# Adding a layer's bias to its nodes by accumulating DMAs of POOL in place of VectorE's additions

## What is computed

```
layer 0:  out = (d * (adj + I) * d) @ x @ W0^T + b0
layer 1:  att[i, j] = softmax_j( p . relu(q[j] + k[i]) + mask(adj) );  out = att @ x      (no bias)
layer 2:  out = (d * (adj + I) * d) @ (x @ W2) + b2
layer 3:  out = (d * adj * d) @ x @ W3 + b3
```

## Time and profile before

| | |
|---|---|
| Median of 3 runs | 14031.23 us (14029.29 to 14034.36) |
| Profiled execution | 14031.93 us, of which the span of the instructions is 14030.1 us |
| TensorE clock granted, mean | 0.982 of full speed |
| DMA | 935.48 MB, all issued by SP; the hardware queue q1 takes 20.9% of the 16 DMA engines |
| HBM | 65 GB/s over the span |

### The profile page before, as it was taken

One profiled execution on the slowest core, in us unless ns is written; L12 is line 12 of the kernel. 1 busy time (PEld: TensorE's weight loads), 2 busy tenths in 40 slices (PEclk: granted clock), 3 DMA queues, 4 the chain that ended last, 5 costly groups with the idle time before them and its releaser, 6 DMA issues. The chain is left out here.

```text
span 14030.1 us, 318060 instructions
## 1 busy us (share of the span) xinstructions
PE 13002.6 (93%) x143877; PEld 5489.3 (39%) x143877; DVE 13269.3 (95%) x13964; ACT 13100.1 (93%) x8612; POOL 1060.3 (8%) x699
## 2 busy tenths in 40 slices
PE   7889989999899998999989999999989999899988
PEld 3333434444344433444334443344433444333333
DVE  6999999999999999999999999999999999999995
ACT  5999999999999999999999999999999999999994
POOL 0000000010000100001000100001000010000000
PEclk8999999999999999999999999999999999999999
DMA  5111112221122111221122211222112221011103
GB/s 187 46 51 47 49 53 83 86 66 51 55 85 90 61 43 62 88 88 58 39 72 86 86 58 40 72 83 87 58 36 75 90 80 58 30 50 52 43 12 109
DMA packets 714332, 935.48 MB, mean 67 GB/s; under 512 B 61712, under 2 KB 455952, under 8 KB 693520
## 3 DMA queue, kind: packets, MB, share of 16 engines
q1 hardware_dynamic: 712976, 915.13, 20.9%
HBM read 722.01 MB, written 184.55 MB: 65 GB/s over the span
## 5 line engine op out<-in xcount | busy, mean ns | idle before, releaser
L1055 DVE TENSOR_SCALAR big<-q_pair,k_pair_cols 128x2048 f32<-128x2048 f32 x10036 | 12122.4, 1283 | 426.5 <-PE score L1203 409.1
L815 ACT ACTIVATE big<-q_f,k_cols 128x2048 f32<-128x2048 f32 x6144 | 11792.8, 1998 | 320.5 <-PE score L1203 275.3
L1203 PE MATMUL score<-big,unit_window 128*32 128x512 f16 x81920 | 5181.7, 396 | 708.5 <-DVE big L1055 674.3
L1203 PE MATMUL score<-big,sign_window 128*32 128x512 f32 x49152 | 5626.6, 598 | 194.9 <-ACT big L815 191.6
L1203 PEld LDWEIGHTS score<-big,unit_window 128*32 128x32 bf16 x81920 | 2292.5, 96 | 3850.2 <-issue 1070.0
L1203 PEld LDWEIGHTS score<-big,sign_window 128*32 128x32 f32 x49152 | 1577.2, 111 | 3520.0 <-issue 3009.7
L1122 PE MATMUL acc<-piece,gs 128*128 128x512 f32 x3072 | 1442.7, 597 | 36.8 <-DVE gs L913 22.4
L625 POOL TENSOR_SCALAR att_var<-att_mom 128x1 f32<-128x1 f32 x128 | 63.8, 498 | 10048.3 <-DVE att_mom L1020 10048.3
L1122 PEld LDWEIGHTS acc<-piece,gs 128*128 128x128 f32 x3072 | 532.7, 191 | 544.7 <-issue 457.8
L1181 PE MATMUL acc<-x,att_turned 128*128 128x128 f32 x4096 | 555.0, 279 | 0.0
L1181 PEld LDWEIGHTS acc<-x,att_turned 128*128 128x128 f32 x4096 | 498.4, 192 | 56.8 <-issue 56.8
(11 more groups left out here) (90 smaller groups left out, 2757.0 us busy)
## 6 DMA issues: line engine op xcount, KB each, us to landing
piece<-adj_turned SPq DMA_DIRECT2D x1536, 256.0 KB, 2.8
att<-in_adj_dram SPq DMA_DIRECT2D x128, 1024.0 KB, 5.2
raw<-in_adj_dram SPq DMA_DIRECT2D x224, 512.0 KB, 4.8
adj_turned<-turned SPq DMA_DIRECT2D x224, 512.0 KB, 5.0
big<-in_adj_dram SPq DMA_DIRECT2D x32, 512.0 KB, 7.5
adj_turned<-big SPq DMA_DIRECT2D x32, 512.0 KB, 6.9
gx<-in_x_dram SPq DMA_DIRECT2D x32, 256.0 KB, 3.9
q_kept<-raw SPq DMA_DIRECT2D x32, 256.0 KB, 3.8
```

What stands on the lines that cost most here:

```text
L815: ins = nc.scalar.activation(ring["A"][:, RANK[g] % RING * 4 + u, :], q_f32[:], ACT.Relu, bias=k_cols[:, t % 2, QUAD * u + g:QUAD * u + g ...
L1055: ins = nc.vector.tensor_scalar(ring["D"][:, RANK[g] % RING * 4 + u, :], q_pair[:], k_pair_cols[:, t % 2, QUAD * u + g:QUAD * u + g + 1], ...
L1203: ins = nc.tensor.matmul(score[QUAD * u:QUAD * (u + 1), cc, :], window[:, QUAD - 1 - g:2 * QUAD - 1 - g], row, start=(g == 0 and part == 0 ...
```

## The change

`add_bias` goes from DVE to POOL. In place of one DVE addition over 128x512 elements, POOL issues one DMA for each step, with `accum_op=ALU.add`: the source is the bias tile of 128x128 in SBUF, read four times over by a stride of 0, and the destination the 4 tiles of `gx`, 128 partitions x 2 KB. The wait for `gs_ready` moves with it. A DMA counts its semaphore up by 16, so `sum_layer` waits for `n * 16`. On POOL the call stands at the same place number, start + 20, ahead of `layer_root` in `side`. No DMA was issued by POOL before.

```diff
--- before.py
+++ after.py
@@ -649,6 +649,13 @@  (POOL)
+            def add_bias(c, name, s):
+                pool.wait_ge(gs_ready, layer_of(c, name) * STEPS + STEPS)
+                tiles = slice(s * PER, (s + 1) * PER)
+                pool.dma_start(gx[:, tiles, :],
+                               bias[name][:].rearrange("p (a f) -> p a f", a=1).broadcast_to([P, PER, D]),
+                               accum_op=ALU.add).then_inc(biased, 16)
+
@@ -665,6 +672,8 @@  (POOL)
             def side(c, place):
+                for name, s in steps_at(c, place, BIAS_AT):
+                    add_bias(c, name, s)
                 for name, s in steps_at(c, place, ROOT_AT):
                     layer_root(c, name, s)
@@ -914,16 +923,9 @@  (DVE)
-            def add_bias(c, name, s):
-                dve.wait_ge(gs_ready, layer_of(c, name) * STEPS + STEPS)
-                tiles = slice(s * PER, (s + 1) * PER)
-                nc.vector.tensor_tensor(gx[:, tiles, :], gx[:, tiles, :],
-                                        bias[name][:].rearrange("p (a f) -> p a f", a=1).broadcast_to([P, PER, D]),
-                                        ALU.add).then_inc(biased, 1)
-
             def sum_layer(c, name, s):
                 n = step_of(c, name, s) + 1
-                dve.wait_ge(biased, n)
+                dve.wait_ge(biased, n * 16)
                 dve.wait_ge(layer_projected, n)
@@ -974,8 +976,6 @@  (DVE)
-                for name, s in steps_at(c, place, BIAS_AT):
-                    add_bias(c, name, s)
```

## The result

The changed kernel takes 14056.01 us (median of 20 runs, 14049.67 to 14063.94), the kernel before 14033.38 us beside it (14029.07 to 14038.89, 20 runs). The ratio is 1.0017, with a 95% interval from 1.001 to 1.0023: 22.6 us slower, more than the noise and less than the 0.2% (28 us) that was set as "no change". Forecast were 14032 us, between 14012 and 14115; the likeliest case's own range, 14015 to 14050, is missed by 6 us.

The account below looks back on a forecast made before the run. No engine alone was taken as the bound, with ACT, DVE and PE all above 92% busy. Removal -6, stalls +2.5 and ends +5 us gave +1.5 on 14031.93, forecast as 14032 us, range 14012 to 14115.

Parts of the forecast that it names:

- likeliest case: Whole kernel: between 14015 and 14050 us whatever the small terms do; chance 0.62.
- Part (1): 96 additions leave DVE's queue; only layer 3's are on the path: 6 us gained, bounds 0 and 11.6.
- fifth rival: DVE's saved time is passed on in more blocks: half of 57.6 us, 14003; chance 0.05.
- Part (2): 96 DMA issues on POOL: within the attention the landing is hidden if issue and landing stay under 50 us.
- third rival: POOL's issue is starved beside DVE's rows and lands past 50 us: 14100 or four times the present; chance 0.08.
- Part (3): POOL's issues beside DVE's tensor_scalar rows within the attention: 0.03 us each, 2.5 us lost.
- second rival: After `rstd` of the step before, an issue holds DVE out 1.0 to 1.97 us: 14085 to 14140; chance 0.20.
- Part (4): Opening and closing: bias DMAs take DMA engine time from loads, 0.4 us in each of 12 steps, 5 us.
- fourth rival: Transfers collide at both ends or contend within the attention: +30 to +67 us, 14060 to 14100; chance 0.05.

Follow-up runs that it names:

- e1: The kernel before without any bias addition, DVE's 96 additions and their wait taken out: 14023.5 us, ratio 0.9995 to the kernel before.
- e7: The changed kernel with its 84 attention biases as 128 pieces of 2 KB from HBM, opening and closing on DVE: 14027.02 us, ratio 0.9995 to before.
- e3: The changed kernel with all 96 bias DMAs reading 128 pieces of 2 KB from HBM: 14053.67 us, ratio 1.0017 to the kernel before.
- e2: The changed kernel with the 12 steps of opening and closing added on DVE again: 14041.89 us, ratio 1.0008 to the kernel before.
- e6: The changed kernel with each bias as two DMAs of 256 pieces: 14054.26 us, ratio 1.0017 to the kernel before.

## Why the prediction was right and wrong

**Part (1), the removal: right.** Forecast were 6 us (0 to 11.6), measured 7.3 in e1 and 8.1 in e7, each with an interval that holds 0 too. In layer 0 the wait came out as read, 1.62 us behind the place of the bias, where 1.6 was forecast from 1.02. In layer 3 the reading "no wait of DVE follows" wasn't right: some 20 us behind the bias the kernel before does wait, 1.35 us, and in the changed one that wait is 1.56 us and a new one of 0.30 us stands before it. So a good part of the time saved turned into waits there as well. The wait of layer 3 before, then the three rows after, the first of them of layer 0:

```profile
2650.03 1.29 DVE L1055 TENSOR_SCALAR big<-q_pair,k_pair_cols 128x2048 f32<-128x2048 f32 x1 [1.35 <-PE score L1203]
```

```profile
6713.68 2.48 DVE L1055 TENSOR_SCALAR big<-q_pair,k_pair_cols 128x2048 f32<-128x2048 f32 x2 [1.62 <-PE score L1203]
...
2636.49 4.87 DVE L1055 TENSOR_SCALAR big<-q_pair,k_pair_cols 128x2048 f32<-128x2048 f32 x4 [0.30 <-PE score L1203]
...
2654.63 9.66 DVE L1055 TENSOR_SCALAR big<-q_pair,k_pair_cols 128x2048 f32<-128x2048 f32 x8 [1.56 <-PE score L1203]
```

DVE's waiting for PE at its score rows went from 409.1 to 444.0 us, 35 us, where 40 to 50 were forecast; in e1, which has no stall, it is 451.3. The fifth rival (the time is passed on in more blocks) is refuted by e1.

**Part (2), the landing: right.** An issue takes 2547 ns on POOL and lands 6.0 us after it begins, 13.3 us at most, where 50 us were free. The third rival, an issue starved for hundreds of microseconds, is refuted.

**Part (3), what POOL does to DVE: this step failed.** It said "the nearest rows give DVE a cost of 0 per issue" and took 0.03 us, 2.5 us in all. Measured are 0.24 us and 18.4 to 20.2 us in all. The rows were right: `var_eps` and `rstd` still cost nothing, as e3 shows with 16.83 us over them and a 128-piece issue. They were the wrong neighbours: each of them touches four elements a partition, and a 512-piece issue is another kind of work. My reading, which no run takes apart, is that the small ones fit into a border between two rows and a part of the issue doesn't. The second rival had this mechanism, place included ("after `rstd` of the step before, where DVE runs 14 tensor_scalars"), but with a price of 1.0 to 1.97 us, a whole instruction of POOL; POOL's instruction did take 2.5 us, and DVE lost a tenth of it. The truth lay between the two values that I had for one issue, below the 0.5 us from which that rival decides. I had discounted layers whose wait hides it, and there I was off as well: 84 x 0.24 = 20.2 us come out nearly whole (18.4), since the stall falls behind the root, where the chain goes through DVE's rows, and not where DVE waits. Had the term been sized from both bounds, a stall of even a quarter of a border (0.3 us) would have given 25 us.

The Trainium skill, "SBUF — State Buffer", section "SBUF: two separate sides", tells of the DMA that is late because DVE holds the shared ports. The trace agrees in that the issue is slower beside DVE's rows (1.33 to 1.51 us in the 12 steps of the ends, 2.1 us and more within the attention), and that delay was worth nothing here. What cost time is the other direction. The rule of its section "Who interferes with whom", the pair held for a whole instruction by whoever is first, doesn't fit DVE's loss if POOL's DMA instruction is taken for that instruction: DVE would have lost up to the 3.12 us of the one at 6650.46 and lost 0.25.

**Part (4), the ends: right in kind, too small.** Forecast were 0.4 us a step, 5 us; measured are 1.3 us a step in the closing and 11.5 to 12.6 us in all (the change against e2). PE's waits for pieces passed the 120 us that I had named as the fourth rival's mark, though 10.9 us of that is a change of label; its price of 30 us and more isn't reached. The argument that the engines are free for 32% of the window counted a mean. The share of q0 above tells the other end: 9.9% of 179 us is 17.7 us for eight DMAs, 2.2 us of all 16 engines each. Of that 1.3 us came through.

**Sum.** The forecast had -6, +2.5 and +5. Measured along before, e1, e2 and the change are -7.3 (removal), +18.4 (stalls) and +11.5 (ends); that these add up to 22.6 is so by construction. What stands on its own is that the stalls read from the score rows, 20.2 us, agree with the 18.4. The sum of +1.5 us was 21 us short. The time lies in the range of 14012 to 14115 only because that range was stretched for the second and the fourth rival, which is what happened in part: an eighth to a quarter of the second's price for an issue, and the near part of the fourth's. That "no change" held, by 5 us, is partly luck.

## What to carry to other kernels

A DMA that an idle engine issues isn't free for its neighbour: count the pieces of its pattern, since here a step from 512 to 128 pieces took the whole stall away. Where the pieces can't be made fewer, put the issue where the neighbour waits anyway; the same 84 stalls, 20 us in sum, cost some 7 us there and 18 us ahead of a chain of full rows. And don't put it where the loads of the same DMA engines set the pace: one change can pay in one stage and cost in another, as e3 did, whose total showed nothing.

## What the runs showed of the hardware

- POOL's DMA issue takes from DVE's stream of 128x2048 `tensor_scalar`: 0.01 us at 128 pieces, 0.17 us at 256 (e6), 0.24 us at 512, 0.60 us at 1024; at 512 the source makes no difference. From 256 on this is 0.5 to 0.7 ns a piece, and at 128 pieces of 2 KB next to nothing. Whether their number or their size makes them free is open.
- An accumulating DMA of 256 KB in 512 pieces takes 2.2 us of the 16 DMA engines (9.9% of 179 us for eight of them, in the closing).
- Open: why the wide form from HBM costs the closing more (2.2 us a step) than the narrow one from SBUF (1.3); its share of the DMA engines there is smaller, as its window of 175 us of the closing shows. No run was made for it.

```profile
q0 software_dynamic: 1152, 2.10, 7.6%
```
